# Ternary feed-forward weights: summed and rounded on ScalarE inside the first attention instead of on VectorE behind it

## The reference, cut to what matters

```python
def weight_quant(w):                       # once per weight matrix: w_gate, w_up [2048, 512], w_down [512, 2048]
    scale = 1.0 / jnp.clip(jnp.mean(jnp.abs(w)), EPS)
    wq = jnp.clip(jnp.round(w * scale), -1.0, 1.0) / scale
    return w + jax.lax.stop_gradient(wq - w)
...
x = x + _L0_xattn_ref(_layernorm(x), ctx, Wq, Wkv, Wout, bout)     # softmax attention, 8 heads of 64
x = x + _L0_ffn_ref(_layernorm(x), w_gate, w_up, w_down)           # gate, up, Hadamard transform, down
x = x + _L1_xattn_ref(...)
x = x + _L1_ffn_ref(...)
```

## Time and profile before

| | us |
|---|---|
| median of three runs | 2618.13 |
| lowest, highest | 2615.9, 2621.28 |
| the profiled execution, its own time | 2617.07 |
| its span, first to last instruction | 2615.3 |
| first attention, to the last residual | 0 to about 877 |
| layer-norm scales | about 877 to 880.3 |
| ternary weights | 880.5 to 964.2 |
| feed-forward layer and the rest | from 964.6 |

### The profile page before, as it was taken

The page is one execution under the profiler, slowest core; times in us unless marked ns, Lnnn a source line. Parts: engine busy times, 40 slices in busy tenths (PEclk is TensorE's granted clock), DMA queues, the critical chain, the costliest instruction groups (busy, mean ns, idle before and its releaser), DMA issues. The chain is left out here.

```text
span 2615.3 us, 35029 instructions
## 1 busy us (share of the span) xinstructions
PE 2049.7 (78%) x11638; PEld 757.2 (29%) x11670; DVE 1586.5 (61%) x2348; ACT 1160.6 (44%) x1639; POOL 1310.5 (50%) x853
## 2 busy tenths in 40 slices
PE   4999999999999206899857888888954209999980
PEld 1222222222222003444422222222213105555540
DVE  5555555555554487676557777777734725565657
ACT  3555555555554015554323666666644004444430
POOL 2666667666677103666413222222212766777750
PEclk8999999999999658999987999999985559999995
DMA  2001000100100527000003223323201025667647
GB/s 94 22 22 34 23 30 22 34 25 28 33 19 26 209 72 203 1 1 1 1 25 59 55 54 59 56 58 59 55 14 66 1 60 177 203 189 208 191 135 321
DMA packets 166276, 192.35 MB, mean 74 GB/s; under 512 B 51014, under 2 KB 123206, under 8 KB 162928
## 3 DMA queue, kind: packets, MB, share of 16 engines
q1 hardware_dynamic: 143008, 151.38, 20.7%
q0 software_dynamic: 17408, 33.67, 3.9%
q10 hardware_dynamic: 5712, 5.45, 0.6%
HBM read 146.97 MB, written 59.93 MB: 79 GB/s over the span
## 5 line engine op out<-in xcount | busy, mean ns | idle before, releaser
L588 DVE TENSOR_REDUCE a_negmax<-a_ps_max 128x2 f32<-128x1024 f32 x256 | 312.2, 1220 | 226.7 <-PE a_ps_max L429 226.6
L1061 DVE TENSOR_REDUCE a_negmax<-a_ps_max 128x1 f32<-128x512 f32 x512 | 333.3, 684 | 119.1 <-PE a_ps_max L909 115.3
L1008 ACT ACTIVATE a_probs<-a_ps_st 128x512 f32<-128x512 f32 x512 | 288.8, 595 | 197.2 <-PE a_ps_st L930 194.9
L542 ACT ACTIVATE a_probs<-a_ps_st 128x1024 f32<-128x1024 f32 x256 | 262.2, 1024 | 232.3 <-PE a_ps_st L449 232.3
L389 POOL TENSOR_TENSOR a_added_up<-a_added_up,a_probs 128x1024 f32<-128x1024 f32 x128 | 301.2, 2353 | 29.9 <-ACT a_probs L542 27.3
L460 PE MATMUL a_ps_o<-a_probs,a_values 128*64 128x512 f32 x1024 | 276.2, 618 | 0.0
L389 POOL TENSOR_TENSOR a_added_up<-a_probs 128x1024 f32<-128x1024 f32 x64 | 150.3, 2349 | 229.4 <-ACT a_probs L542 229.4
L909 PE MATMUL a_ps_max<-a_k_st,a_q_st 96*128 96x512 f16 x512 | 201.5, 394 | 9.5 <-DVE a_negmax L1061 6.7
L930 PE MATMUL a_ps_st<-a_q_st,a_k_st 97*128 97x512 f16 x512 | 196.8, 387 | 8.1 <-ACT a_probs L1008 2.5
L43 PE MATMUL s_gu<-s_xT,s_gu_h 128*128 128x384 f16 x768 | 188.7, 328 | 1.9 <-DVE s_xT L2165 1.9
L581 DVE SCALAR_TENSOR_TENSOR a_qk_l<-a_ps_misc,a_qk_h 128x512 f16<-128x512 f32 x122 | 84.4, 692 | 137.3 <-ACT a_qk_h L525 137.3
(11 more groups left out here) (412 smaller groups left out, 4251.3 us busy)
## 6 DMA issues: line engine op xcount, KB each, us to landing
s_raw<-in_guT SPq DMA_DIRECT2D x32, 768.0 KB, 5.7
a_inverse<-a_dram_inverse SPq DMA_DIRECT2D x128, 128.0 KB, 2.9
m_y_tok<-f_nothing SPq DMA_DIRECT2D x16, 1024.0 KB, 10.1
c_yg<-m_y_tok SPq DMA_DIRECT2D x16, 1024.0 KB, 8.0
a_ctx_in<-in_ctx SPq DMA_DIRECT2D x32, 256.0 KB, 3.0
s_raw<-in_dnT SPq DMA_DIRECT2D x32, 256.0 KB, 6.0
s_raw<-in_dnT SPq DMA_DIRECT2D x64, 128.0 KB, 6.6
a_q_st<-a_dram_halves SPq DMA_DIRECT2D x48, 128.0 KB, 3.7
```

What stands on the lines that cost most here:

```text
L542: act.activation(probs[:, s % RING, :, :], ps_st[:, :, :], ACT.Exp).then_inc(exped, 1)
L588: dve.tensor_reduce(negmax[:, v % 2, :, i % KD], ps_max[:, :, :], AX.X, ALU.max, negate=True).then_inc(maxed, 1)
L1008: act.activation(probs[:, s // HG % 3, s % HG, :], ps_st[:, s % 2, :], ACT.Exp, scale=DH1 ** -0.5).then_inc(exped, 1)
L1061: dve.tensor_reduce(negmax[:, g % 2, at:at + 1], ps_max[:, i % 2, :], AX.X, ALU.max, negate=True).then_inc(maxed, 1)
```

## The change

`quantise_weights` goes. In its place the 256 steps of the first attention carry 96 chunks of 128 partitions by 512 columns: 48 in a first pass (sum of absolute values, at even steps 16 to 110), 48 in a second (rounding, at even steps 128 to 222). Each chunk is loaded twice, by SyncE at the iteration three steps ahead, into one of three slots. The rounding uses the fused multiply and add of a large constant, and then Sign instead of a clip. To make room in memory, three rings shrink: probabilities from 6 to 5, running sums from four head pairs to three, queries and keys from eight head pairs to seven.

```diff
+    RING = 5
+    CHUNKS = 3 * KD * FF // D
+    PER = CHUNKS // 3
+    SLOTS = 3
+    UPS = 3
+    QK = 7
+    SUMMED_FROM, ROUNDED_FROM = STEPS, 8 * STEPS
+    MEANS_AT = 7 * STEPS + 2
...
+        ones = sb("ones", [P, P], F32)
+        magic = sb("magic", [P, 2], F32)
+        w_raw = sb("w_raw", [P, SLOTS, D], F32)
...
+            def load_chunk(m):
+                need(sp, w_used, m - SLOTS + 1)
+                w, c = m % CHUNKS // PER, m % PER
+                src = d[("wgT", "wuT", "wdT")[w]]
+                cols = src.shape[1] // D
+                sp.dma_start(w_raw[:, m % SLOTS, :], src[P * (c // cols):P * (c // cols) + P, D * (c % cols):D * (c % cols) + D]).then_inc(w_in[m % SLOTS], 16)
...
             for s in range(T):
                 g = s // 8 - 1
+                if chunk_at(s + 3) is not None:
+                    load_chunk(chunk_at(s + 3))
                 if s % KD == 2 and s // KD + 1 < KD * B:
                     place_maxima(s // KD + 1)
...
-                total = added_up[:, v // 2 % 2, 2 * (v % 2):2 * (v % 2) + 2, :]
+                total = added_up[:, v % UPS, :, :]
                 if j == 1:
-                    need(pool, summed, v // 2 - 1)
+                    need(pool, summed, (v - UPS) // 2 + 1)
...
+            def total_weights():
+                pe.wait_ge(w_step, 1)
+                pe.wait_ge(maxrow, MEANS_AT // KD + 3)
+                need(pe, sums_kept, MEANS_AT // 8)
+                nc.tensor.matmul(ps_tr[:, 0:3], ones[:, :], w_sums[:, :], start=True, stop=True).then_inc(w_total, 1)
...
+                if s == MEANS_AT + 4:
+                    total_weights()
+                if s == MEANS_AT + 5:
+                    pe.wait_ge(w_step, 3)
...
+            def chunk(m):
+                w, c = m % CHUNKS // PER, m % PER
+                raw_w, out_w = w_raw[:, m % SLOTS, :], wq[:, w, D * c:D * c + D]
+                act.wait_ge(w_in[m % SLOTS], 16 * (m // SLOTS + 1))
+                if m < CHUNKS:
+                    act.activation(out_w, raw_w, ACT.Abs, accum_out=w_part[:, m:m + 1]).then_inc(w_used, 1)
+                else:
+                    act.wait_ge(w_step, 3)
+                    act.activation(raw_w, raw_w, ACT.Identity, bias=magic[:, 0:1], scale=w_inv[:, w:w + 1]).then_inc(w_rounded, 1)
+
+            def chunk_sign(m):
+                w, c = m % CHUNKS // PER, m % PER
+                act.wait_ge(w_rounded, m - CHUNKS + 1)
+                act.activation(wq[:, w, D * c:D * c + D], w_raw[:, m % SLOTS, :], ACT.Sign, bias=magic[:, 1:2], scale=1.0).then_inc(w_used, 1)
...
                 exponential(s)
+                if chunk_at(s) is not None:
+                    chunk(chunk_at(s))
+                if s > ROUNDED_FROM and chunk_at(s - 1) is not None:
+                    chunk_sign(chunk_at(s - 1))
                 if s % 8 == 4 and s > 8:
                     keep_sums(s // 8 - 1)
...
+            def weight_sums():
+                dve.wait_ge(w_used, CHUNKS)
+                dve.tensor_reduce(w_sums[:, :], w_part[:, :].rearrange("p (w c) -> p w c", w=3), AX.X, ALU.add).then_inc(w_step, 1)
+
+            def weight_means():
+                dve.wait_ge(w_total, 1)
+                dve.tensor_scalar(means[:, :], ps_tr[:, 0:3], 1.0 / (D * FF), Q_EPS, ALU.mult, ALU.max).then_inc(w_step, 1)
+                dve.wait_ge(w_step, 2)
+                dve.reciprocal(w_inv[:, :], means[:, :]).then_inc(w_step, 1)
...
+                if s == MEANS_AT:
+                    weight_sums()
+                if s == MEANS_AT + 5:
+                    weight_means()
...
-        quantise_weights(nc, wq, means, d)
```

More of the change, by code:

```diff
@@ L293, in first_attention @@
                  "weighted kept added summed sums_kept sums_out compact_in recip inverse_out inverse_in normalised out_proj residual").split())
+        w_in = [sem(f"w_in{q}") for q in range(SLOTS)]
+        w_used, w_rounded, w_step, w_total = (sem(n) for n in ("w_used", "w_rounded", "w_step", "w_total"))
         def first_context(sp):
@@ L366, in _ @@
             sp.wait_ge(rows_in, 32 * KD * B)
+            for q in range(SLOTS):
+                sp.wait_ge(w_in[q], 16 * 2 * CHUNKS // SLOTS)
             sp.wait_ge(inverse_in, 16 * HG * GROUPS)
@@ L428, in max_products @@
                 for half, rows in enumerate(HALVES):
-                    last = nc.tensor.matmul(ps_max[:, half, :], qk_h[rows, n % 2, 2 * u, P * t:P * t + P], qk_h[rows, n % 2, 2 * u + 1, :],
+                    last = nc.tensor.matmul(ps_max[:, half, :], qk_h[rows, i // KD % QK, 0, P * t:P * t + P], qk_h[rows, i // KD % QK, 1, :],
                                             start=True, stop=True)
@@ L469, in sum_up @@
                     at = P // HG * hh
-                    last = nc.tensor.matmul(ps_tr[at:at + P // HG, :], ones[:, :], added_up[:, g % 2, hh, :], start=True, stop=True)
+                    last = nc.tensor.matmul(ps_tr[at:at + P // HG, :], ones[:, 0:P // HG], added_up[:, (2 * g + hh // 2) % UPS, hh % 2, :], start=True, stop=True)
                 last.then_inc(summed, 1)
@@ L523, in evacuate @@
                 if t < 8:
-                    need(act, scores, STEPS * (n - 1))
-                    act.activation(qk_h[:, n % 2, t, :], bank, ACT.Copy, scale=1 / WS).then_inc(evac_high, 1)
+                    v = KD * n + t // 2
+                    need(act, scores, KD * (v - QK + 1))
+                    act.activation(qk_h[:, v % QK, t % 2, :], bank, ACT.Copy, scale=1 / WS).then_inc(evac_high, 1)
                 else:
```

90 lines of the change are left out of this document (25 added, 65 removed).

## The result

| | median, us | lowest to highest | ratio to before, 95% interval |
|---|---|---|---|
| before, same job | 2618.05 | 2615.9 to 2621.28 (4 runs) | |
| changed | 2539.98 | 2537.6 to 2547.25 (4 runs) | 0.9707 [0.9690, 0.9723] |
| changed, repeated in another job | 2538.22 | 2536.89 to 2540.59 (5 runs) | 0.9696 [0.9683, 0.9710] |

The kernel is 78 to 79 us faster (before measured 2617.14 in the job of the repeat, 15 runs).

What follows compares the result with a forecast made beforehand. TensorE was taken to pace the attention, with the VectorE-only stage behind it wholly on the path. 2617.1 - 84.0 + 0.6 + 0.3 + 0.2 = 2534.2, plus 1.1 to the median: 2535 us; range 2531 to 2548.

Steps and rivals of the forecast that it cites:

- Removed, 84.03 us, less 1.1: Between first attention and feed-forward layer: the VectorE stage's 84.03 us all saved, less 0.6 + 0.3 + 0.2 us added.
- the means: In the first attention: a matmul on three columns, +0.6 us, and TensorE waiting for two small VectorE instructions, +0.3 us.
- ScalarE, 113 us added and 0 on the path: First attention: 48 x (0.84 + 0.80 + 0.72) us more busy time on ScalarE, hidden by idle time and slack, 0 us paid.
- the evacuation is late by up to 0.38 us at s % 8 = 4: Projection-tile evacuation on ScalarE: added work against 0.46 us idle; 0.38 idle before the next exponential and 0.77 slack absorb it.
- The slack behind the gap: First attention: VectorE's low part ends 0.77 us before TensorE loads the next projection's weights, cover beyond ScalarE's idle time.
- Given back in part: Rival, first attention: loops absorb less, or loads delay rows of maxima; 2540 to 2562 us, about 2550; chance 0.14.
- ScalarE sets the pace: Rival, first attention: added ScalarE work beyond gap and slack, from 1.7 us, lengthens steps in full; 2648 us; chance 0.02.
- Table loads, smaller rings, loads: First attention: no extra table loads, smaller rings without waits, 96 SyncE loads of 256 KB in time; each 0 us.
- The rest from the feed-forward layer on is the same within 3 us: Feed-forward layer to kernel end: 1650.7 us before; the prediction counted as wrong if this changed by more than 3 us.
- the clock 2 us to either side: Feed-forward layer's start: TensorE's clock neither gained nor lost, 0 us; where its rise falls may move the time 2 us.
- the partial rival: The rival of savings given back in part in the first attention, 2540 to 2562 us; chance 0.14.

## Why the prediction was right, and where it was not

**Removed, 84.03 us, less 1.1: right.** 82.94 us in the repeat (82.93 forecast). That the two agree to 0.01 is luck: with unchanged batches the feed-forward layer starts anywhere between 880.5 and 882.1 us, and the 1.1 were themselves too high, as the means below show. No time is given back in the attention: with the old stage put back, the time is that of before within 3.1 us.

**ScalarE, 113 us added and 0 on the path: right,** at 111.8 us and batches of 51.19. Its reasoning was right in kind and too tight in size. The step "the evacuation is late by up to 0.38 us at s % 8 = 4" measured 0.02 with an Abs (321.30 - 319.30 = 2.00 against 1.98) and 0.13 with an Identity (475.12 - 473.01), and the plain step keeps 0.34 and 0.25 us of its gap instead of 0.11 and 0.15. Durations had been laid end to end, while successive rows of ScalarE overlap by 0.10 us. 192 added instructions make that 19 of the 21.5 us by which idle time fell less than busy time rose. The slack behind the gap, 0.77 us, measured 0.83.

**"Given back in part": refuted.** Another Abs in each of 48 steps costs 0; one three times as long costs 1.27 us a batch, 7.6 in all. The rival "ScalarE sets the pace" begins later than the 1.7 us named: a plain step that carried 1.47 + 0.62 + 0.19 us of rows paid 0 to 0.2.

**The Trainium skill's rule** ("ScalarE: Activation LUTs", section "Rules for kernel authors": VectorE, not ScalarE, for simple arithmetic) has no say in the time here: 111.8 us on ScalarE replace 71.5 on VectorE, and none of the 111.8 is on the path. The Trainium skill's estimate in the same section for an ACTIVATE with a bias in memory, about 0.3 us and 0.83 ns for each element, makes 0.72 us of 512 columns; the trace agrees, the Sign measured 712 ns.

**Table loads, smaller rings, loads: 0, right.** No load of tables stands between exponential, Sign and Identity, and the traces have 10 rows of table loads before and after alike; a ring of 4 is as good as 5; the chunks land in 2.8 to 3.1 us with no wait for them, and of the three steps two can be spared for 1.2 us.

**The means, 0.9 us: too high.** Their batch took 51.33 us instead of 51.19, so 0.14.

**"The rest from the feed-forward layer on is the same within 3 us": this step failed.** It took 1650.7 us before, 1663.2 in the first trace and 1657.0 in the repeat. Of the 12.5 us in the first, 5.7 are in the feed-forward layer, where the forecast gave the clock 2 us to either side: that term was mis-sized for a single execution. 2.9 are at the end, and the rest is 0.7 to 2.4 us in each of three stages, about as much as they differ between repeats (up to 2.0). The forecast had no term for the end. The kernel without the old stage waits 2.7 to 3.3 us for TensorE's last instruction, and with nine idle instructions added it does not; then the rest is 2529.7 - 880.9 = 1648.8 us, within 3 of before. That the wait comes from moving what stands behind the removed code is the likely reading, and its cause is open. Without this cost the changed kernel measures 2531.82, with it 2538 to 2540, and the forecast of 2535 lies between. Of this difference only 3.3 us are located at the end, so a forecast nearer than that would have been luck.

**The range.** By its own terms its low end is 2535.3 - 2 - 3 = 2530.3 us, not 2531, and the lower half of the partial rival, 2540 to 2562, reaches to 2551, not 2548. Nothing hangs on either: the medians lie inside both.

## What to carry to other kernels

A serial stage that depends on none of its neighbour's data can be worth its whole length when it moves into the idle gaps of an engine there, as here; count the gap and the slack behind it, and count added instructions from start to start, not by their row's length. To learn how much an engine can still carry, put work that changes nothing into each step and watch the time of a batch, not the total: the totals of one kernel lie 4 to 10 us apart here, the batches of the loaded stretch 0.01. And when a total misses by a few microseconds after code was removed, compare the very end of both traces before blaming the part that was edited.

## What the runs showed of the hardware that was not expected

- **Rows of ScalarE overlap.** The next instruction begins 0.10 us before the row of the last one ends. This holds for the accumulator's read too: it begins at 313.84, before the Abs row ends at 313.94, and in the tight step what follows it begins 0.09 us after it, though its row is 0.19 long. The Trainium skill ("Perfetto Trace Analysis", section "DVE / Act Engine Instruction") says that a row ends when the memory has acknowledged the last write, and that the next instruction may start its reads once the execution is over. The overlap of these rows agrees with that; the acknowledgement itself no row shows.
- **An accumulated sum is an instruction of its own,** 193 ns, of which 0.09 us count towards what follows.
- **The end of the program.** The branch that jumps over a large block takes TensorE 3.4 to 4.1 us, and its last instruction comes another 2.7 to 3.3 us late (nine traces) or not at all (five), depending on a few instructions far ahead of it. VectorE shows a wait of the same kind behind its own branch, 2.8 to 2.9 us against 0.6, but in the kernels with the old stage. That it is the fetching of code is a guess; what the traces show is the wait, and that instructions far ahead change it.
- **A copy on GpSimd beside VectorE.** The same instruction on VectorE (128x16) took 1.80 us while GpSimd converted a constant, and 0.17 us when that had not begun.
- **The clock in a broken-up layer.** The same kernel's feed-forward layer took 389.1 and 384.1 us in two executions of one program, with 0.66 and 0.87 granted in the same 40 us. What decided it the traces do not tell.
